# ScalarE takes a quarter of the layer-norm statistics; variance and root move to later in the round

## The reference

```python
xn = layernorm(x)                       # per token, over 512 values
D = fractal_dimension(xn)               # from the first 1024 values: one number
x1 = real(ifft(fft(xn) * filter(D)))    # a circular filter along the 512 values
bits = sigmoid(x1 @ W_el + b_el) > 0.5  # 24 bits a token
s = x1 + golay_correct(bits) @ W_le + b_le
p = softmax(xn @ router_w.T)            # 8 experts
top = top_k(p, 2); w = top.values / (top.values.sum() + 1e-6)
ffn = sum over the 2 of (xn @ expert[e] + p_e) * w_e
out = x + s * silu(ffn)
```

## Time and profile before

| | |
|---|---|
| time, median of 3 runs | 1230.14 us (1227.67 to 1231.77) |
| the profiled execution's own time | 1231.95 us |
| its span, first to last instruction | 1230.1 us |
| busy PE / DVE / POOL / ACT | 1127.8 / 1099.3 / 875.6 / 511.8 us |
| DMA queue 1 / queue 0, share of 16 engines | 42.5% / 21.9% |
| mean granted PE clock | 0.971 |

### The profile page before, as it was taken

How to read it: one execution, slowest core, us unless ns; L and a number is a source line. 1 busy time by engine, 2 the same in 40 slices (tenths; PEclk the granted TensorE clock), 3 DMA queues, 4 the chain that set the end, 5 groups by cost and what they waited for, 6 DMA issues and landing times. The chain is left out here.

```text
span 1230.1 us, 26833 instructions
## 1 busy us (share of the span) xinstructions
PE 1127.8 (92%) x6283; PEld 607.8 (49%) x6284; DVE 1099.3 (89%) x2664; ACT 511.8 (42%) x1151; POOL 875.6 (71%) x857
## 2 busy tenths in 40 slices
PE   5998988725888999999999999999999999999996
PEld 4554544412443555555555554555555555555553
DVE  6799998888886889899999998999999899999985
ACT  4576665564664333333333333333333333333332
POOL 1126655648885678788888877888888788888874
PEclk9999999957999999999999999999999999999998
DMA  8658999413455676667666666666666666666663
GB/s 324 241 194 217 216 178 175 67 31 95 146 164 157 154 174 173 165 178 176 171 172 174 177 174 168 169 178 174 172 172 172 173 179 173 168 176 174 174 168 108
DMA packets 216921, 208.74 MB, mean 170 GB/s; under 512 B 166271, under 2 KB 166271, under 8 KB 212786
## 3 DMA queue, kind: packets, MB, share of 16 engines
q1 hardware_dynamic: 184370, 124.31, 42.5%
q0 software_dynamic: 31360, 79.78, 21.9%
q10 hardware_dynamic: 1152, 4.19, 1.3%
HBM read 123.36 MB, written 47.11 MB: 139 GB/s over the span
## 5 line engine op out<-in xcount | busy, mean ns | idle before, releaser
L1425 PE MATMUL banks<-w_hi,arena 128*128 (+1 forms) x1136 | 432.3, 381 | 9.0 <-DMA arena<-arena 4.3
L1426 PE MATMUL banks<-w_lo,arena 128*128 (+1 forms) x1136 | 431.9, 380 | 0.0
L1427 PE MATMUL banks<-w_hi,arena 128*128 (+1 forms) x1136 | 431.7, 380 | 0.0
L711 ACT ACTIVATE arena<-xbuf,inf 128x512 f16<-128x512 f32 x156 | 112.6, 722 | 531.3 <-DVE xbuf L1215 531.0
L524 POOL DMA_INDIRECT xbuf<-in_L_attn_x,gidx x156 | 187.4, 1201 | 78.1 <-issue 65.6
L526 POOL DMA_INDIRECT inf<-token_info,gidx x156 | 202.7, 1299 | 54.1 <-issue 52.5
L503 POOL DMA_INDIRECT pair_tokens<-tok,slot x112 | 109.6, 978 | 112.8 <-DVE slot L1050 80.8
L564 POOL TENSOR_TENSOR xbuf<-xbuf 128x512 f32<-128x512 f32 x128 | 162.7, 1271 | 34.5 <-DVE xbuf L1284 26.9
L1425 PEld LDWEIGHTS banks<-w_hi,arena 128*128 128x128 f16 x1136 | 111.3, 98 | 137.8 <-issue 15.6
L1427 PEld LDWEIGHTS banks<-w_hi,arena 128*128 128x128 f16 x1136 | 111.5, 98 | 130.9 <-issue 1.6
L530 POOL DMA_INDIRECT out<-xbuf,sidx x128 | 142.7, 1115 | 40.7 <-issue 40.4
(11 more groups left out here) (304 smaller groups left out, 1741.6 us busy)
## 6 DMA issues: line engine op xcount, KB each, us to landing
xbuf<-in_L_attn_x SPq DMA_DIRECT2D x32, 1024.0 KB, 11.9
arena<-extra_sums SPq DMA_DIRECT2D x128, 256.0 KB, 2.7
arena<-in_L_ffn_expert_weights SPq DMA_DIRECT2D x8, 1024.0 KB, 11.0
extra_sums<-arena SPq DMA_DIRECT2D x28, 256.0 KB, 2.1
token_info<-info ACTq DMA_DIRECT2D x8, 512.0 KB, 8.9
xbuf<-in_L_attn_x,gidx POOLq DMA_INDIRECT x156, 3.6
inf<-token_info,gidx POOLq DMA_INDIRECT x156, 2.9
arena<-arena SPq DMA_TRANSPOSE x128
```

Source lines behind the costliest of these rows:

```text
L711: nc.scalar.activation(hi4[ring(i, k)], uv2[:, b], ACT.Copy, scale=inf2[:, k, 1:2]).then_inc(hi_ready, 1)
L1425: mm(ps, hi[:, c], wh, start=(c == 0), stop=False)
L1426: mm(ps, hi[:, c], wl, start=False, stop=False)
L1427: end = mm(ps, lo[:, c], wh, start=False, stop=(c == C - 1))
```

## The change

Of each x load the fourth tile's statistics leave DVE. ACT makes them in two passes over the tile, both with an accumulated output: a copy scaled by 1/512 gives the mean (`tile_mean`), and a square of mean minus x gives the sum of squared deviations (`tile_square`). They stand on both sides of `latT_copy` in the step ahead of the tile's own. The bf16 result of both passes is thrown away into `inf2`. After the fourth load of a round one small copy of the four means follows (`pairs_alike`). The slot of a load is free only when ACT's square is done too.

`deviations` moves from k = 1 to k = 2, behind `halves` and `place`, and waits for ACT's sums. The root moves on ACT from the end of step k = 2 to the start of step k = 3, ahead of all copies. The three statistics of load (i + 1, 0) come after `deviations`, no longer beside `place`, and the last links of `choose` have nothing beside them. In `weigh` the Newton steps start two links later. In round 0 the `halves` of expert 2 come before the Newton steps, not after them.

After phase one the first `low_sums` stands ahead of DVE's wait for `toks_mm`, and ACT makes the turned copies of extras 0 and 1 ahead of the high part of extra 2.

```diff
             def load(i, k):
                 after(sp, t1_done, GT * ((i - 1) * U + k + 1))
                 after(sp, stats_ready, (i - 1) * U + k + 1)
+                after(sp, squares_ready, (i - 1) * U + k + 1)
                 sp.dma_start(xbuf[:, k], x_tiles[:, i, k * GT:(k + 1) * GT, :]).then_inc(ld_x[k], 16)
...
+            def tile_mean(i, k):
+                act.wait_ge(ld_x[k], 16 * (i + 1))
+                if k == 0:
+                    after(act, var_ready, i)
+                after(act, squares_ready, i * U + k)
+                nc.scalar.activation(squares, xbuf[:, k, GT - 1], ACT.Copy, scale=1.0 / E,
+                                     accum_out=last_st[:, k, 1:2]).then_inc(means_ready, 1)
+
+            def tile_square(i, k):
+                act.wait_ge(means_ready, i * U + k + 1)
+                nc.scalar.activation(squares, xbuf[:, k, GT - 1], ACT.Square, bias=last_st[:, k, 1:2], scale=-1.0,
+                                     accum_out=last_st[:, k, 2:3]).then_inc(squares_ready, 1)
+                if k == U - 1:
+                    nc.scalar.activation(last_st[:, :, 4], last_st[:, :, 1], ACT.Copy).then_inc(pairs_alike, 1)
+
             def step1(i, k, last):
                 ahead = not (last and k + 1 >= U)
+                if k == 3:
+                    act.wait_ge(var_ready, i + 1)
+                    nc.scalar.activation(rt1[:, 1], rt1[:, 0], ACT.Sqrt).then_inc(sd_ready, 1)
                 if ahead and not turned_early(i, k):
                     turn_copy(*at(i, k, 1), 0)
                     turn_copy(*at(i, k, 1), 1)
+                if (i, k) == (0, 0):
+                    tile_mean(0, 0)
+                    tile_square(0, 0)
+                if ahead:
+                    tile_mean(*at(i, k, 1))
                 latT_copy(i, k)
+                if ahead:
+                    tile_square(*at(i, k, 1))
...
-                if k == 2:
-                    act.wait_ge(var_ready, i + 1)
-                    nc.scalar.activation(rt1[:, 1], rt1[:, 0], ACT.Sqrt).then_inc(sd_ready, 1)
-                    if i >= 1:
-                        bits_copy(i - 1)
+                if k == 2 and i >= 1:
+                    bits_copy(i - 1)
...
             def extra_step(n):
                 k, b = n % U, n % 2
-                if n + 1 < NX:
+                if 0 < n < NX - 1:
                     turned_copy(n + 1)
...
                 gather_index(1, k)
-            turned_copy(0)
+                if k == 1:
+                    turned_copy(0)
+                    turned_copy(1)
...
-                if q == GT - 1:
+                if q == GT - 2:
                     ins.then_inc(stats_ready, 1)
...
             def deviations(i):
                 dve.wait_ge(stats_ready, U * (i + 1))
+                dve.wait_ge(squares_ready, U * (i + 1))
+                dve.wait_ge(pairs_alike, i + 1)
...
-                return [lambda q=q: stat(i, k, q) for q in range(GT)]
+                return [lambda q=q: stat(i, k, q) for q in range(GT - 1)]
...
-                    choose(i - 1, beside=tiles_of(i, 1) + tiles_of(i, 2) + tiles_of(i, 3))
+                    choose(i - 1, beside=tiles_of(i, 1) + tiles_of(i, 2) + tiles_of(i, 3) + NONE)
...
-                    deviations(i)
                     if i + 2 < NE:
                         halves(i + 2 if i else 1)
                 if i >= 1 and k == 2:
-                    place(i - 1, (i - 1) % 2, (i - 1) // 2, beside=following)
+                    place(i - 1, (i - 1) % 2, (i - 1) // 2)
+                if k == 2:
+                    deviations(i)
+                    for tile in following if i else []:
+                        tile()
                 if k == 3:
                     if i >= 1:
-                        weigh(i - 1, beside=newton_steps(i))
+                        weigh(i - 1, beside=[None, None] + newton_steps(i) + [None])
                     else:
-                        for step in following + newton_steps(i):
+                        for step in following:
                             step()
                         halves(2)
+                        for step in newton_steps(i):
+                            step()
...
+            low_sums(0)
             dve.wait_ge(toks_mm, 1)
...
             last.then_inc(live_ready, 1)
-            low_sums(0)
```

More of the change, by code:

```diff
@@ L245, in build @@
             "p (t s e) -> p t s e", s=2, e=NE)
+        squares = inf2[:, :, :].rearrange("p k w -> p (k w)").bitcast(BF16)
+        last_st = st6[:, :, :].rearrange("p (k q) c -> p k q c", k=U)[:, :, GT - 1]
         info_bits = info[:, :, 16:64].bitcast(BF16).rearrange("p t (g c) -> p t g c", g=3)
@@ L300, in build @@
             "t1_done t1_copied mm1_done latT_copied back_done lat_copied")
+        means_ready, squares_ready, pairs_alike = sems("means_ready squares_ready pairs_alike")
         stats_ready, aggr_ready, var_ready, sd_ready, newton, rstd_ready = sems(
@@ L873, in _ @@
             V.tensor_copy(iota_h[:, :], iota_c)
+            V.memset(last_st[:, :, 5], 0.0)
             V.tensor_copy(used[:, :], region_c).then_inc(sort_init, 1)
@@ L935, in deviations @@
                 V.tensor_tensor(rt1[:, 0], dev[:, 1], dev[:, 3], ALU.add).then_inc(var_ready, 1)
-            NONE = [None] * (U - 1) * GT
+            NONE = [None] * 12
             def newton_steps(i):
@@ L1024, in weigh @@
                 lk(V.tensor_scalar(den, den, 1e-6, None, ALU.add), beside[4])
-                lk(V.reciprocal(den, den))
-                lk(V.tensor_tensor(w12, p12, each(den, 2), ALU.mult))
+                lk(V.reciprocal(den, den), beside[5])
+                lk(V.tensor_tensor(w12, p12, each(den, 2), ALU.mult), beside[6])
                 V.tensor_tensor(p12, p12, w12, ALU.mult)
@@ L1061, in step1 @@
             def step1(i, k, last):
-                following = NONE if last else tiles_of(i + 1, 0)
+                following = [] if last else tiles_of(i + 1, 0)
                 if i >= 1 and k == 0:
-                    choose(i - 1, beside=tiles_of(i, 1) + tiles_of(i, 2) + tiles_of(i, 3))
+                    choose(i - 1, beside=tiles_of(i, 1) + tiles_of(i, 2) + tiles_of(i, 3) + NONE)
                 if (i, k) == (R - 1, 1):
```

## The result

The changed kernel takes **1240.46 us** (1238.73 to 1244.56), the kernel before 1230.13 us: a ratio of 1.0081, 95% interval 1.0058 to 1.0105. It is 10.3 us slower; I had forecast 1224.0 us, 6 faster. The profiled execution took 1244.56 us with a span of 1242.7, 12.6 over the span of before.

What follows compares the result with a forecast made beforehand. DVE was taken to pace phase one's middle rounds, DMA those from about 150 us. Round 0 and rounds 1 to 3 win 6.5 us, less 0.8, plus 0.5: 6.2 off 1230.1 gives 1224 us, range 1217.5 to 1230.5.

Steps and rivals of the forecast that it cites:

- The sizes of the parts: Phase one: `choose` with 9 statistics 11.5 us, `place` 3.95, an ACT pass 0.65, ACT 23.2 us a round.
- DVE's round of 25.2 us: Middle rounds of phase one: DVE's round falls from 26.68 to 25.20 us, 1.48 us less.
- the circle: From one round's logits through ACT and DVE to the next round's: closes at 24.8 us, DVE at 25.2 still later.
- my DVE branch: Ranks 0.5, `place` 3.95, `deviations` 0.8 ahead of the root; 9.4 us from logits (i, 2) to logits (i + 1, 0).
- The PE step: Each PE step of phase one grows from 5.69 to about 5.95 us, the square joining ACT's chain.
- Round 0: `halves` of expert 2 fill DVE's wait for the root; `choose` starts at 54.9, not 57.02: 2.1 us less.
- The last round: PE sets the end; `deviations`, now behind `place`, is no longer hidden under DVE's wait for ranks: 0.8 us more.
- Round 6: Late in phase one: counted among 6 rounds that would each win 1.48 us with DMA out of the way.
- After phase one: First `low_sums` goes into DVE's wait for `tile_tok`, at most 1.2 us gained; taken as 0.5 us less.
- The cap by DMA: From about 150 us DMA sets rounds of 26.6 to 27.0 us, cutting the gain from 10.7 to 6.2 us.
- The slower rival: ACT becomes the bound: `bits_copy` waits for the store in rounds 3 to 6, 14.8 us against 10.7 gained: 1234; 8%.

Runs made afterwards that it cites:

- one bits copy: Changed kernel with one of ACT's three copies of the bits, the other bits not stored: 1230.28 us, 0.9999 of the kernel before.
- passes left out: Changed kernel without ACT's statistics passes and the waits for them, the fourth tile's statistics being constants: 1226.96 us, 0.9971 of the kernel before.
- filler: Changed kernel with 16 overwritten matmuls of 128 columns in PE's wait at k = 3 of each round: 1230.76 us, 1.0015 of the kernel before.
- two loads: Changed kernel with ACT's passes for loads k = 1 and k = 2 alone, deviations and root at their old places: 1222.0 us, 0.9935.
- only the tail edited: Kernel before with only the two edits behind phase one: 1229.14 us, 0.9997 of the kernel before.
- the one with before's tail: Changed kernel without the two edits behind phase one: 1237.38 us, 1.0064 of the kernel before.

## Why the prediction was wrong

**The sizes of the parts were right.** `choose` with nine statistics takes 11.42 us (forecast 11.5), `place` 3.94 (3.95). A pass costs 0.61 us of the queue for the mean and 0.71 for the square, read of the accumulator included (0.65 each); the two are 1.32 us of ACT for the 0.60 of one statistic on DVE. ACT is busy 22.7 us a round (23.2). DVE's round of 25.2 us shows where nothing else is slower: from `pairs` to `pairs` 25.15 us with one bits copy (121.33 to 146.48) and with the passes left out (117.98 to 143.13). From the root on, the circle takes 3.9 us (136.44 to 140.32), as forecast.

**The step that failed is the circle, 24.8 us, "DVE at 25.2 still is later".** I followed it from the ranks through DVE (0.5, 3.95, 0.8), and wrote 0.3 for the root. ACT is an in-order queue, and ahead of the root in it stand the last `latT_copy`, square, `pairs_alike`, two copies, three bits copies (2.36 us) and a table load (1.30 us): 5.9 us from 130.40, so that the root came at 136.32, while DVE had done its part at 135.6. I had named what queues behind the root and not what queues ahead of it. The bits copies had their row (2.37 us), and the table load was in before's trace too. The kernel with one bits copy shows my DVE branch by itself: 9.48 us for the forecast 9.4.

The PE step was 6.07 us, not 5.95, which adds 0.24. Together: 25.8 us in place of 25.2, so 0.8 us a round under before, not 1.48.

**Missed altogether: the clock.** No sentence of the prediction asks what PE's new idle time does. In the profile of after it takes some 9 us of phase one in five rounds, and the filler gives back some 10 us. The Trainium skill, "TensorE: Matmul & The Clock Gate", Part 1, warns of just this, that waits between bursts of matmuls bring the gate down to half rate. The runs agree that it happens (0.50 of the clock at 113 us), but its advice, which goes by the length of the gap, doesn't sort them: 1.25 us was followed by a fall at 111.17 and not at 138.65, and 3.03 us was not. Nor is every fall a cost, as before's at 124 us shows.

**Round 0: 2.1 us less, in truth 4.7 more.** I took the norm's load as landed at the same time and the root at 52.1. It came at 53.87, and behind it, as in all rounds, `latT_copy` waits; the step again looked only at DVE. PE's `turn_back` comes 2.5 us later than before (56.21, 53.70); of the other 2.2 us, 1.7 is the clock. Where ACT's queue was not made longer, the forecast held: with two loads `choose` starts at 54.26, for the forecast 54.9.

**The last round: 0.8 us more, measured 1.2** (15.32 to 16.50), with no passes too (16.3 us). **Round 6 was counted as one of six that win 1.48 us.** It has no `halves`, so no DVE round of 26.6 us either: it takes 24.2 with before's phase one and 28.3 in after. **After phase one: 0.5 us less, measured nothing** (0.9997). `tile_tok` to the main rounds takes 128.2 us before and 129.2 after, and 127 to 130 in the other kernels with either tail.

**The cap by DMA, which cut 10.7 us to 6.2, was no cap.** It rested on 20.0 us to landing in the earlier trace rows and a share of 1.04. With the same phase one and only the tail edited, loads between 150 and 204 us land in 10.4 us and the rounds are 26.6 us; the long queue belonged to that one execution. Rounds of 25.1 us at a share of 1.02 (one bits copy) and of 25.8 at 1.01 (filler) show that such a share is no floor of 26.6 us. So had the circle held, the likelier error would have been too small a gain.

**The slower rival** had a true mechanism and the wrong weight. `bits_copy` did wait for the store with the root behind it (1.92 us at 186.26), once, not in each of four rounds, and cost 2.0 us of PE's time; slower came from the queue ahead of the root and the clock, which no rival had.

## What to carry to other kernels

When an instruction with a wait is moved on an in-order engine, sum both branches up to it: what it waits for, and all that stands ahead of it on its own queue, table loads included. The later one counts. A microsecond of new idle time on TensorE can cost another 1.7 us through the clock if the round waits for PE, and nothing if it doesn't, so ask of a new PE wait what it does to the clock and who waits for PE then; a few useless matmuls in it tell at once. If an engine is relieved by another that has "room", try a smaller part with the order left as it was: two loads of four with the root at its old place gave -8 us, where four with a late root gave +10. And cut a round at the engine that bounds it: cut at another, the windows show that engine's catching up.

## What the runs showed of the hardware

- The clock fell after PE waits of 1.25 to 3.29 us and held after others of 1.25, 1.95 and 2.14, and after four of 3.0 us, in stretches where PE runs the same instructions. With the same phase one it fell in rounds 0, 1, 2, 5 and 6 of the changed kernel, and in rounds 0, 4, 5 and 6 of the one with before's tail. What decides is not settled; no run here varied it by itself.
- The read of an accumulator takes 0.09 to 0.10 us of ACT's queue (131.51 to 131.60), though its row shows 0.19. The square, whose bias comes from memory, takes 0.61 us up to that read (130.90 to 131.51) and the mean, a copy, 0.52 (137.39 to 137.91); no run tells whether the 0.09 between them is the bias or the function.
- The table load takes 1.28 us in its row and the next instruction starts 1.30 us after it. The changed kernel has as many table loads as the one before, so its passes needed none of their own.
- In one comparison the kernels, the one before too, were some 7% slower, with stops of 4 to 8 us on PE and ACT, some of which the profile ascribes to nothing. The kernel with one bits copy stood at 1.0133 there and at 0.9999 elsewhere, so a ratio from such runs can't be carried over. The cause is open.
